# A decoder kernel whose second attention projects queries and keys once, by token, and turns them after the rotation

## What is computed

```
q = einsum('bsd,hkd->bhsk', x, wq);  k = ... wk;  v = ... wv      # 16 heads of 16
x * cos + swapped * sin            # swapped: (-x1, x0) in each pair of features, for q and k
scores = einsum('bhqk,bhsk->bhqs', q, k) / sqrt(16);  causal mask;  softmax
out = einsum('bhqs,bhsv->bqhv', attn, v) @ wo.T
```

## Time and profile before

| | us |
|---|---|
| median of 3 runs (995.99 to 1000.39) | 997.88 |
| the profiled execution, its own time | 996.32 |
| its span in the trace | 993.8 |
| TensorE busy | 933.5 |
| VectorE busy | 615.2 |
| ScalarE busy | 421.7 |
| POOL busy | 117.3 |

### The profile page before, as it was taken

How to read it: one execution, slowest core, us unless ns; L and a number is a source line. 1 busy time by engine, 2 the same in 40 slices (tenths; PEclk the granted TensorE clock), 3 DMA queues, 4 the chain that set the end, 5 groups by cost and what they waited for, 6 DMA issues and landing times.

```text
span 993.8 us, 14098 instructions
## 1 busy us (share of the span) xinstructions
PE 933.5 (94%) x5348; PEld 717.9 (72%) x5348; DVE 615.2 (62%) x1148; ACT 421.7 (42%) x1053; POOL 117.3 (12%) x136
## 2 busy tenths in 40 slices
PE   7998689999999998999988999999997899999997
PEld 5665367888888786666766777777774678888886
DVE  3445555666666643566657868778684656666664
ACT  4535244334443412878334434434333443333342
POOL 2101100000000044000123222223220000000000
PEclk9897779999999998999999999999999899999999
DMA  5000031111110040000510000000000311111001
GB/s 191 2 1 1 1 128 48 48 48 47 47 32 1 0 170 0 2 2 1 223 65 1 1 1 1 1 1 1 1 1 15 114 49 49 50 52 54 17 1 43
DMA packets 12249, 37.55 MB, mean 38 GB/s; under 512 B 1921, under 2 KB 4065, under 8 KB 11297
## 3 DMA queue, kind: packets, MB, share of 16 engines
q1 hardware_dynamic: 12160, 36.78, 11.0%
q0 software_dynamic: 32, 0.01, 0.0%
HBM read 35.73 MB, written 1.05 MB: 37 GB/s over the span
## 4 chain that ended last, share of the span: by engine, by line
PE 87%; ACT 7%; DVE 4%; issue 1%; DMA 0%; POOL 0%; SPq 0%; ACTq 0%; DVEq 0%
PE ps L1074 80%; PE ps L1570 3%; PE ps L1219 2%; ACT Q L904 2%; DVE xn L405 1%; PE ps L1085 0%; DVE stats L397 0%; ACT probs_q L985 0%; DMA xb_w<-in_xb_w 0%; PE ps L1358 0%; ACT DT L767 0%; ACT whi L919 0%; DVE X L449 0%; ACT lnvar L760 0%; DVE rope_buf L650 0%
## 5 line engine op out<-in xcount | busy, mean ns | idle before, releaser
L942 ACT ACTIVATE h_hi<-weighted_h 128x512 fp32r<-128x512 f32 x100 | 63.2, 632 | 157.7 <-DVE weighted_h L569 157.7
L1074 PE MATMUL ps<-xTh,whi 128*128 128x512 f32 x400 | 125.2, 394 | 1.8 <-ACT silu_g L940 1.8
L1074 PE MATMUL ps<-xTh,wlo 128*128 128x512 f32 x400 | 123.4, 390 | 0.0
L1074 PE MATMUL ps<-xTl,whi 128*128 128x512 f32 x400 | 123.2, 389 | 0.0
L571 DVE TENSOR_TENSOR h_lo<-weighted_h,h_hi 128x512 fp32r<-128x512 f32 x100 | 69.3, 693 | 69.7 <-ACT h_hi L942 69.7
L566 DVE TENSOR_TENSOR shared_gate<-silu_g,row_shares 128x512 f32<-128x512 f32 x88 | 60.9, 692 | 62.3 <-ACT silu_g L940 62.2
L1074 PE MATMUL ps<-xT,merged_q 128*128 128x256 f32 x384 | 92.3, 384 | 1.7 <-DVE rope_buf L651 1.7
L940 ACT ACTIVATE silu_g<-ps 128x512 f32<-128x512 f32 x100 | 59.6, 596 | 78.1 <-PE ps L1074 78.0
L1066 POOL TENSOR_TENSOR latent_rot<-rope_buf 128x256 f32<-128x256 f32 x96 | 68.6, 736 | 187.9 <-DVE rope_buf L651 187.9
L1074 PEld LDWEIGHTS ps<-xTh,whi 128*128 128x128 f32 x400 | 74.6, 189 | 19.3 <-issue 4.5
L1074 PEld LDWEIGHTS ps<-xTh,wlo 128*128 128x128 f32 x400 | 75.5, 189 | 16.0
(11 more groups left out here) (185 smaller groups left out, 1572.6 us busy)
## 6 DMA issues: line engine op xcount, KB each, us to landing
raw<-in_ffn SPq DMA_DIRECT2D x50, 384.0 KB, 3.1
wx<-in_wx SPq DMA_DIRECT2D x4, 2048.0 KB, 9.8
cx<-in_cx SPq DMA_DIRECT2D x1, 1536.0 KB, 9.5
wqkv<-in_wqkv SPq DMA_DIRECT2D x1, 1280.0 KB, 8.4
X<-in_x SPq DMA_DIRECT2D x4, 256.0 KB, 4.8
rope_buf<-in_kvc SPq DMA_DIRECT2D x1, 1024.0 KB, 4.8
out<-X SPq DMA_DIRECT2D x4, 256.0 KB, 2.2
wqkv<-in_wqkv SPq DMA_DIRECT2D x1, 512.0 KB, 5.3
```

The lines of the kernel that those rows point to most:

```text
L942: a.activation(h_hi[:, u % 2, :], weighted_h[:, u % 2, :], ACT.Copy).then_inc(act_hi[l], 1)
L1074: return pe.matmul(o, l, r, start=start, stop=stop, skip_group_check=True)
```

## The change

Attention 1 projects queries and keys once each, with tokens on the partitions, into banks 4 and 5 or 0 and 1 by turns. VectorE multiplies with the cosines in one instruction, and with the sines in two that read every second feature and write beside it. POOL adds the two products, nothing more. TensorE then turns the sum (`turned`, eight 128x128 transposes a sequence, banks 2 and 3), one sequence behind the projections, and for the last sequence after step 1 of the scores; ScalarE copies the turned queries to `qT` and the turned keys, with a scale by partition, to `kE` and `kO`. The first score step waits until VectorE has read banks 4 and 5. The weights with swapped columns, `kT` and the wide tables fall away. `sg` has two halves. `kvc` gets its own memory and is loaded with the first two groups of cross weights; of the tables the larger part is loaded first; VectorE rotates the shared keys after the `merged_s` of group 2. In period 3 of attention 0 the preload moves from ahead of `norm(1, b - 1)` to ahead of `root(b - 1)`. The experts' last results go through banks 2 and 3 in place of 5 and 4.

```diff
-            for j, tab in enumerate(("cos", "sin", "cos", "sin")):      # project1
-                v.wait_ge(pe_f, 4 * b + j + 1)
...
+            for j in range(2):
+                v.wait_ge(pe_f, 2 * b + j + 1)
+                if b >= 2:
+                    v.wait_ge(pe_turn, 2 * (b - 2) + j + 1)
...
+                v.tensor_tensor(along, x, cos.to_broadcast([P, 2, HEADS, HD]), ALU.mult).then_inc(rope_done, 1)
+                for e in range(2):
+                    v.tensor_tensor(across[:, :, :, e::2], x[:, :, :, 1 - e::2], sin[:, :, :, e::2].to_broadcast([P, 2, HEADS, HD // 2]), ALU.mult).then_inc(rope_done, 1)
...
-            if 1 <= b <= NB:                                            # ScalarE, attention 0
-                if c < NB:
+                if c <= NB:
                     a.preload_act_table_set(LN_EXP)
                 root(b - 1)
...
-                if c <= NB:
+                if c < NB:
                     a.preload_act_table_set(LN_EXP)
                 norm(1, b - 1)
...
+        def turned(b):                                                  # ScalarE
+            a.wait_ge(pe_turn, 2 * b + 1)
+            a.activation(qT[:, b].rearrange("p m s -> p (m s)"), ps[:, 2, :], ACT.Copy).then_inc(q_ready, 1)
+            a.wait_ge(pe_turn, 2 * b + 2)
+            for half, sign in ((kE, "even_s"), (kO, "odd_s")):
+                a.activation(half[:, b].rearrange("p m s -> p (m s)"), ps[:, 3, :], ACT.Identity, scale=k(sign)).then_inc(k_ready, 1)
...
-            g.tensor_tensor(kT[:, :, :].rearrange("p m s -> p (m s)"), sg[:, 2, :], sg[:, 3, :], ALU.add).then_inc(k_sum, 1)
-            g.tensor_scalar(kE[:, b], kT[:, :, :], k("even_s"), None, ALU.mult).then_inc(k_ready, 1)
-            g.tensor_scalar(kO[:, b], kT[:, :, :], k("odd_s"), None, ALU.mult).then_inc(k_ready, 1)
+            for j, done in enumerate((q_sum, k_sum)):
+                g.wait_ge(rope_done, 6 * b + 3 * j + 3)
+                g.tensor_tensor(sg[:, b % 2, 2 * j, :], sg[:, b % 2, 2 * j, :], sg[:, b % 2, 2 * j + 1, :], ALU.add).then_inc(done, 1)
...
+                    last = pe.transpose(ps[:, 2 + j, ...], sg[:, b % 2, 2 * j, ...], ident)   # TensorE, turned(b)
+                last.then_inc(pe_turn, 1)
...
-                tokens(1, 6, 4, b).then_inc(pe_v, 1)
-                for j in range(4):
-                    if b >= 1:
-                        pe.wait_ge(rope_done, 4 * (b - 1) + j + 1)
-                    features(1, j, j, b).then_inc(pe_f, 1)
+                tokens(1, 6, 2, b).then_inc(pe_v, 1)
+                for j in range(2):
+                    if b >= 2:
+                        pe.wait_ge(rope_done, 6 * (b - 2) + 3 * j + 3)
+                    tokens(1, rope_bank(b, j), j, b).then_inc(pe_f, 1)
+                if b >= 1:
+                    turned(b - 1)
...
+                        if n == 1:
+                            turned(NB - 1)
...
                             if n == 2:
-                                pe.wait_ge(rope_done, 4 * NB)
+                                pe.wait_ge(q_ready, 2 * NB)
+                                pe.wait_ge(k_ready, 4 * NB)
                             transposed_probabilities(n - 2)
```

More of the change, by code:

```diff
@@ L206, in build @@
                 wx = sb("wx", [P, 2, XPACK], c=weights)
+                kvc = sb("kvc", [P, 2, NB, SEQ], c=weights)
             kvh = sb("kvh", [P, NB, SEQ], F32R, c=phase)
@@ L279, in build, with rope_bank @@
         RECIPROCAL_BANK = 1
+        def rope_bank(b, j):
+            return 4 * ((b + 1) % 2) + j
         PIECE_BANK = dict(x=2, q=0, k=2, v=0, g1=2, gate=0)
@@ L314, in y_bank @@
         def y_bank(t):
-            return (7, 0, 5, 4)[t // 2]
+            return (7, 0, 2, 3)[t // 2]
         def blocks(eng):
@@ L655, in cross @@
                     if hg == 2:
-                        v.wait_ge(kvc_in, 32)
-                        for j, tab in enumerate(("coskv", "sinkv")):
-                            v.tensor_tensor(kvc[:, j, :, :], kvc[:, j, :, :], kx(tab).unsqueeze(1).to_broadcast([P, NB, SEQ]), ALU.mult).then_inc(kv_products, 1)
-                        v.wait_ge(kv_products, 2)
-                        v.tensor_tensor(kvT[:, :, :], kvc[:, 0, :, :], kvc[:, 1, :, :], ALU.add).then_inc(kv_rotated, 1)
-                        v.wait_ge(kv_rotated, 1)
                         v.wait_ge(cx_in, 16)
@@ L674, in cross @@
                                             gm[:, j, e:e + 1], None, ALU.mult).then_inc(merged_s_copied, 1)
+                    if hg == 2:
+                        v.wait_ge(kvc_in, 32)
+                        for j, tab in enumerate(("coskv", "sinkv")):
+                            v.tensor_tensor(kvc[:, j, :, :], kvc[:, j, :, :], kx(tab).unsqueeze(1).to_broadcast([P, NB, SEQ]), ALU.mult).then_inc(kv_products, 1)
+                        v.wait_ge(kv_products, 2)
+                        v.tensor_tensor(kvT[:, :, :], kvc[:, 0, :, :], kvc[:, 1, :, :], ALU.add).then_inc(kv_rotated, 1)
                 v.wait_ge(pe_kv_tokens, 1)
@@ L1185, in scores_by_key, with turned @@
                 last.then_inc(pe_s, 1)
+            def turned(b):
+                for j, summed in enumerate((q_sum, k_sum)):
+                    pe.wait_ge(summed, b + 1)
+                    if b >= 1 and j == 0:
+                        pe.wait_ge(q_ready, NB + b)
+                    if b >= 1 and j == 1:
+                        pe.wait_ge(k_ready, 2 * (NB + b))
+                    for m in range(2):
+                        for t in range(2):
+                            last = pe.transpose(ps[:, 2 + j, 256 * m + 128 * t:256 * m + 128 * t + 128], sg[:, b % 2, 2 * j, 256 * t + 128 * m:256 * t + 128 * m + 128], ident)
+                    last.then_inc(pe_turn, 1)
             def scores_by_query(n):
@@ L1652, in constants @@
     put("block_ones", (p[:, None] // HD) == (p[None] // HD))
-    dd = p % HD
+    dd = np.arange(HD)
     inv = np.float32(10000.0) ** (-(np.arange(0, HD, 2, dtype=np.float32) / np.float32(HD)))
-    ang = (q.astype(np.float32)[None] * inv[dd // 2][:, None]).astype(np.float32)
+    position = (p[:, None] + P * np.arange(2)[None]).astype(np.float32)
+    ang = (position[:, :, None] * inv[dd // 2][None, None]).astype(np.float32)
     put("cos", np.cos(ang))
-    put("sin", np.where(dd[:, None] % 2 == 0, -1.0, 1.0) * np.sin(ang))
+    put("sin", np.where(dd % 2 == 0, -1.0, 1.0) * np.sin(ang))
     r = p[:, None]
@@ L1752, in lay_out @@
         "xb_b": np.broadcast_to(i["L0_xattn_b"].reshape(1, 1), (P, 1)),
-        "wqkv1": np.stack([rows_to_lhs(w.T) for w in (wq, wq[swap], wk, wk[swap], wv)], axis=1),
+        "wqkv1": np.stack([rows_to_lhs(w.T) for w in (wq, wk, wv)], axis=1),
         "gate0": router_columns(i["L0_ffn_gate_w"]),
```

37 lines of the change are left out of this document (15 added, 22 removed).

## The result

The changed kernel takes 992.71 us (median of 20 executions, 982.53 to 994.85), the kernel before 997.2 in the same comparison (991.64 to 1000.93). The ratio is 0.9938, with an interval of 0.9916 to 0.9960: 4.5 us faster, where 13.9 were forecast, and above the end of the range, 989.5. The executions of the changed kernel fall in two groups: nine at 982.5 to 988.6 us, with a mean granted clock of 0.962 to 0.969, and eleven at 992.7 to 994.9 with 0.955 to 0.957. The profiled one (its own time 992.71, span 990.5) is of the second.

What follows compares the result with a forecast made beforehand. TensorE, busy for 94% of the span, was taken to bound the kernel. Terms 11.0 + 0 + 2.1 + 0.8 = 13.9 us off 997.9 gave 984.0 us; own range 981 to 987, 8-in-10 range 980 to 989.5.

Steps and rivals of the forecast that it cites:

- Projections: Attention 1 projections: fewer query and key matmuls, less added transposes, take 11.0 us off the path (bounds 10.7 and 11.2).
- the covers: Attention 1 projections: waits for VectorE's products and POOL's sums are hidden by other TensorE work; without that, at most 2.8 us, four times.
- The first steps: First score steps of attention 1, with three added ScalarE copies: 0, between a gain of 2.0 and a loss of 1.5 us.
- first rival: Attention 1 steps: low clock lasts 10 us longer, half of that at most lost, 5 us: 989; chance 0.09.
- Cross: Cross: rotating the shared keys later starts group 2 2.1 us earlier, leaving one wait of 1.4 us.
- Attention 0: Period 3 of attention 0: four of five table loads go, gaining TensorE's wait of 0.78 us, taken as 0.8 (bounds 0 and 1.5).
- Transposes: Attention 1 projections: rival that each transpose costs its record's length, 0.28 us, giving 987.7; chance 0.04.
- Tables: ScalarE's turned copies: rival that the scaled copy needs another table, two loads of 1.28 us each time, giving 986.6; chance 0.04.
- Strided products: Attention 1 projections: rival that VectorE's reads of every second word set the pace, slower than before; chance 0.03.
- x: Time of each of VectorE's four every-second-word instructions a sequence; binds from 1.28 us, the whole gain is gone from 2.15.
- the last two rivals: Attention 1 projections: VectorE's strided reads set the pace (chance 0.03), or the projections don't shorten, giving 995 (chance 0.02).
- the VectorE rival: Attention 1 projections: VectorE's reads of every second word set the pace; 1003.5 us at 2.5 us per instruction; chance 0.03.

Runs made afterwards that it cites:

- a_bank: Changed kernel, sequence 3 turned into banks 0 and 1 and copied behind step 6, so no second idle time; 982.0 us, ratio to before 0.9876.
- a_oldload: Changed kernel with the table preload of attention 0, period 3, put back where it stood before; 990.7 us, ratio to before 0.9942.
- a_fill: Changed kernel with both idle times filled by repeated query matmuls of sequence 3, results not used; 980.0 us, ratio to before 0.9849.
- a_late: Changed kernel, both idle times left, eight query matmuls of 256 columns (results not used) added ahead of score step 3; 983.1 us, ratio to before 0.9880.
- a_fill1: Changed kernel with only the first idle time filled by repeated query matmuls, results not used; 979.2 us, ratio to before 0.9824.
- a_fill2: Changed kernel with only the second idle time filled by repeated query matmuls, results not used; 981.4 us, ratio to before 0.9834.
- a_fillold: Changed kernel with both idle times filled by repeated query matmuls and the attention 0 preload put back as before; 980.6 us, ratio to before 0.9855.
- a_vlate: Changed kernel with sequence 3's value matmuls moved from the projections into the first idle time, nothing done twice; 982.3 us, ratio to before 0.9850.
- b_copies: Kernel before, with three unused ScalarE copies after the exponentials of step 1 that step 0's transposes wait for; 997.8 us, ratio to before 1.0025.

## Why the prediction was wrong

**Projections: right.** Per sequence the groups cost 1.73 and the transposes 0.87, the lower bound given. The stage gained 9.9 us, not 11.0, since the first sequence ran its three groups partly at a clock of 0.50, until about 349.4 us (6.43 us in place of 5.19, 1.2 us); in the traces of a_bank and a_oldload, which don't have that, the stage takes 24.2, 11.2 less than before, the upper bound given. The wait on `pe_turn`, the new wait of score step 0 and POOL's sums held nobody up, as the covers had it.

**The first steps: the step that failed.** The term was 0, between a gain of 2.0 and a loss of 1.5 us. The idle times (1.9 and 2.0 us forecast, 1.85 and 2.05 measured), the copies and the start of the transposes at +9.5 came out. So did the upper end: at 1.00 the steps take 93.6 us in a_fill, 1.9 less than before, where 2.0 was given. The other end, 1.5 us of loss, was worked out as if the low clock would last as before. Measured was a loss of 11.9 us in the trace of the change, and of 3.7 in that of a_oldload, the only one of the faster group: both are beyond it. The prediction named the danger, as its first rival, and mis-sized it twice. It let the low clock last 10 us longer than before, and it lasted 24 longer. It priced the loss at half of 10, with a chance of 0.09; 11 of 20 executions are in the slower group. The reason it gave against, that TensorE gets through 1.68 and 1.47 us in cross at 1.00, took idle times with heavy work around them (128-row matmuls of 256 columns) for a guide to idle times amid 32-row score matmuls. a_late shows that what stands behind an idle time counts, a_fill1 and a_fill2 that the pair counts; in cross itself neither was tried. The price by length held as a bound: half of the low time was given, and 34 us (with 3.4 more in the window from 430 to 440, at 0.83) cost 13.9.

**Cross: right**, 1.95 us against 2.1; the wait that is left is 1.47 us against 1.4. `merged_s` of group 3 starts 27.93 us after the start of the merged weights, before 29.78: 1.85 earlier where group 2 is 1.95 earlier, so 0.1 us late (0.3 was forecast).

**Attention 0: within its bounds, not shown at its size.** The traces differ by 3.8 us there, but 1.9 of these were there before period 3, and the clock is low at 25 to 28.5 us in this execution and at 34 to 40.5 in the one before. The pair of a_fill and a_fillold shows no gain in its traces and 0.6 us within the noise in its medians; 0.8 was forecast. The forecast took the end of TensorE's work at 89.92 as fixed, but that work ran at a clock of 0.50 from about 85. Where it runs at 1.00 TensorE is there 3.2 us ahead of ScalarE's old chain (8.0 against 11.19), so the upper bound of 1.5 was too low.

**The other rivals fell.** Transposes: 0.87 for eight, not 2.2. Tables: the copies with Identity stand some 0.5 us apart with no load between them. The page "ScalarE: Activation LUTs" of the Trainium skill (section "Table sets: the hidden batching unit") says that copy and identity are in every set, and the trace agrees. Strided products: x is 0.39 us, not over the 0.42 of a 128x256 instruction. The page "Vector Engine (DVE) Microarchitecture Reference" of the Trainium skill, section 5.2, gives 1.71 to 2.51 ns per column where one or more of the streams step or hop at every element, against 1.054 where all are contiguous; it has no row for a step of two words or for a source in PSUM. An estimate from that page is 0.42 us and 256 times the difference, 0.6 to 0.8 us. The trace does not agree, and the measurement, 0.39 us, decides.

**The chances** have a slip: all but the last two rivals make 0.95, not 0.94, and two thirds of the VectorE rival make 0.02 for slower, not 0.03.

**The sum at an equal clock.** With the gain end of the first steps it is 11.0 + 2.0 + 2.1 + 0.8 = 15.9, so 981.3 us; a_fill takes 980.0. Part of that agreement is luck. In the traces the three stages of attention 1 and cross give 13.8 us where 15.1 were forecast, and attention 0 gives 3.5 by where its low clock lies, not the 0.8 of the loads. Likewise the nine executions of the change at 982.5 to 988.6 us lie in the range of 980 to 989.5, and its median does not: whether the forecast came out hung on how long the low clock lasts behind two idle times, for which the prediction had no row.

**What stays open.** Why the same code runs through the low stretch in some 14 us in one execution and in 34 in another is not shown; in the two traces the clock falls 7.2 and 7.8 us after the first scores, just before and just after the second idle time begins, and nothing was tried on that. Nor is it shown why one execution of a_bank takes 991 us, one of a_late 993, and one each of a_fill and a_fillold 988. Behind its eight records in the first idle time and with 2.05 us of the second, a_vlate loses the clock three times where a_fill1, with the same rows there, keeps it; they differ in what stands ahead. That it takes both idle times for the long stretch is what a_fill1, a_fill2 and a_bank show for this place, one trace each; the one idle time of 2.88 us in the kernel before gave 10 us only, and the one attempt to make the pair elsewhere (b_copies) did not produce the idle times.

## What to carry to other kernels

A change that takes work off TensorE can lose what it gains when it leaves short idle times in a stretch of light matmuls, so look at the granted clock behind every idle time that the change makes or moves, and price a fall by its longest stretch, not by that of the old trace. Put work that is due anyway, and heavy, into such an idle time (a value projection here), or move what the next step waits for out of the way; here one of two neighbouring idle times was enough. Where two profiled executions differ in a stage that the change hardly touches, compare their low windows first, and measure the step in two traces with the low clock at the same places. What a step off the critical path is worth can hang on the clock too: the same preload gained nothing at 0.50 and, by the estimate above, would gain some 3 us at 1.00.

## What the hardware did that was not expected

- Two idle times of 1.85 and 2.05 us with a 1.5 us score step between them were followed by 34 us at 1.2 GHz (14 in another execution) in which TensorE, once at work again, was busy without a break. With either of them filled with eight records of 128x256 it was some 3 us at a time or none.
- At a clock of 0.50 TensorE is busy for 10.00 of 10 us and the busy share hides the loss: 50 instructions in the window, and 73 at 1.00 with 8.82 us busy (a_fill).
- With 5.1 us of heavy matmuls behind the fall the clock was back at 1.00 after some 7 us in place of 34, and the kernel with them was 9.6 us faster than the one without.
- VectorE reads PSUM with a step of two features at no extra cost in this form: 0.39 us for 128x256, against 0.42 at unit step.
- Five table loads on ScalarE, 1.28 us each, cost TensorE nothing while its own work beside them ran at 0.50: `output(0, 1)` starts 11.19 us after the `ps<-sq` product with them (a_fillold) and 11.21 without four of them (a_fill).
